# Leaky ReLU of a feed-forward with one operand taken from PSUM, in two halves

## The reference

```python
# layer 0, after a deformable convolution with 4 groups x 9 points, a batch norm and a gate s
x3 = x2 * s[:, None, None, :]
hmid = jax.nn.leaky_relu(jnp.einsum('nhwc,oc->nhwo', x3, fc1_w) + fc1_b, SLOPE)   # 256 -> 1024, SLOPE = 0.01
m = jnp.einsum('nhwc,oc->nhwo', hmid, fc2_w) + fc2_b                              # 1024 -> 256
return (inp + m).transpose(0, 3, 1, 2)
```

## Time and profile before

| | |
|---|---|
| median of 3 runs | 7485.81 us (7482.09 to 7492.41) |
| the profiled execution | 7487.15 us |
| its span, from the first to the last instruction | 7485.3 us |
| mean granted TensorE clock (1 is 2.4 GHz) | 0.745 |
| VectorE busy | 5173.2 us, 69% |
| GpSimd busy | 4751.4 us, 63% |
| TensorE busy | 3828.6 us, 51% |
| ACT busy | 1072.8 us, 14% |

### The profile page before, as it was taken

One profiled execution on the slowest core, in us unless ns is written; L12 is line 12 of the kernel. 1 busy time (PEld: TensorE's weight loads), 2 busy tenths in 40 slices (PEclk: granted clock), 3 DMA queues, 4 the chain that ended last, 5 costly groups with the idle time before them and its releaser, 6 DMA issues.

```text
span 7485.3 us, 45646 instructions
## 1 busy us (share of the span) xinstructions
PE 3828.6 (51%) x10560; PEld 2011.8 (27%) x10560; DVE 5173.2 (69%) x5212; ACT 1072.8 (14%) x1619; POOL 4751.4 (63%) x4676
## 2 busy tenths in 40 slices
PE   5243142351475526632764346426656652589957
PEld 3121021220232214411322124213223431234523
DVE  3778778786777768866777679767777975432545
ACT  1110100000111002211110022101001210121333
POOL 0577777777777777777777777777777777200000
PEclk9666576675687767866887678768878876799978
DMA  6373563754433333355333333553333355201067
GB/s 167 109 206 98 178 183 99 220 149 138 148 122 124 101 103 116 123 203 173 122 123 113 103 111 123 191 181 128 122 113 105 122 175 178 79 34 36 34 177 166
DMA packets 681090, 991.26 MB, mean 132 GB/s; under 512 B 413984, under 2 KB 483616, under 8 KB 665248
## 3 DMA queue, kind: packets, MB, share of 16 engines
q0 software_dynamic: 221184, 604.27, 25.2%
q1 hardware_dynamic: 459808, 385.87, 17.2%
HBM read 792.21 MB, written 197.59 MB: 132 GB/s over the span
## 4 chain that ended last, share of the span: by engine, by line
POOL 49%; issue 22%; PE 13%; DVE 9%; DMA 4%; SPq 2%; ACT 1%; DVEq 0%; POOLq 0%; ACTq 0%
POOL ring L369 48%; PE PS L690 12%; DVE ring L1337 3%; DVE dbuf L1343 2%; DMA img<-d_dram 2%; DMA ring<-table,idx_stage 1%; SPq L483 1%; ACT img L1059 1%; DMA cb<-o_dram 1%; DVE sm L1749 0%; DMA o_dram<-img 0%; POOL idx_stage L385 0%; DMA d_dram<-dbuf 0%; SPq L618 0%; SPq L639 0%
## 5 line engine op out<-in xcount | busy, mean ns | idle before, releaser
L369 POOL DMA_INDIRECT ring<-table,idx_stage x4608 | 4720.1, 1024 | 1435.2 <-issue 1370.1
L1343 DVE TENSOR_REDUCE dbuf<-ring 128x64 f32<-128x2304 f32 x512 | 2070.1, 4043 | 45.9 <-DMA d_dram<-dbuf 18.4
L1337 DVE TENSOR_TENSOR ring<-ring,wt 128x576 f32<-128x576 f32 x2048 | 1414.0, 752 | 973.7 <-DMA ring<-table,idx_stage 855.1
L690 PE MATMUL PS<-img,wb_sb 128*128 128x512 f32 (+1 forms) x3328 | 1646.8, 656 | 468.9 <-DVE img L1402 296.4
L690 PE MATMUL PS<-img,wa_sb 128*128 (+1 forms) x1984 | 931.4, 631 | 666.5 <-DVE img L1723 248.3
L690 PEld LDWEIGHTS PS<-img,wb_sb 128*128 128x128 f32 x3328 | 694.9, 213 | 1387.0 <-issue 1098.4
L690 PEld LDWEIGHTS PS<-img,wa_sb 128*128 128x128 f32 x1984 | 398.4, 203 | 1170.1 <-issue 1079.3
L690 PE MATMUL PS<-sm,params 128*128 128x4 f32 (+1 forms) x32 | 9.1, 355 | 863.1 <-DVE sm L1381 762.0
L690 PE MATMUL PS<-wa_sb,cb 128*128 128x108 f32 (+1 forms) x1024 | 238.8, 399 | 371.8 <-DVE cb L1402 371.8
L787 PE MATMUL PS<-params,img 128*128 128x128 f32 x256 | 62.9, 427 | 689.1 <-DMA img<-d_dram 689.1
L1059 ACT ACTIVATE img<-PS,sm 128x512 f32<-128x512 f32 x384 | 247.5, 680 | 1092.9 <-PE PS L690 1092.9
(11 more groups left out here) (191 smaller groups left out, 2977.5 us busy)
## 6 DMA issues: line engine op xcount, KB each, us to landing
ring<-table,idx_stage POOLq DMA_INDIRECT x4608, 2.9
table<-cb SPq DMA_DIRECT2D x128, 512.0 KB, 7.3
img<-y_dram SPq DMA_DIRECT2D x64, 512.0 KB, 6.6
q_dram<-img SPq DMA_DIRECT2D x32, 1024.0 KB, 4.3
img<-q_dram SPq DMA_DIRECT2D x32, 1024.0 KB, 6.9
img<-in_x SPq DMA_DIRECT2D x8, 2048.0 KB, 12.2
y_dram<-cb SPq DMA_DIRECT2D x64, 256.0 KB, 3.0
d_dram<-dbuf SPq DMA_DIRECT2D x128, 128.0 KB
```

What stands on the lines that cost most here:

```text
L369: nc.gpsimd.indirect_dma_start(out=ring[:, g, p * CORNERS * GC:(p + 1) * CORNERS * GC], out_offset=None, in_=tab[b], in_offset=bass.Indire ...
L690: return nc.tensor.matmul(o, l, r, start=start, stop=stop, **kw)
L1337: last = vec.tensor_tensor(rg, rg, weights.unsqueeze(2).to_broadcast([P, n, GC]), ALU.mult)
L1343: vec.tensor_reduce(dbuf[:, j, g * GC:(g + 1) * GC], ring[:, g, :].rearrange("p (k c) -> p c k", c=GC), AX_X, ALU.add).then_inc(sem("ring_ ...
```

## The change

ACT writes 0.01 (z + b) in place of z + b: it takes `fb_low` = 0.01 `fb` as its bias and 0.01 as its scale. VectorE then takes z itself from PSUM, adds `fb` and writes the larger of that and ACT's value, bank by bank, so in two instructions of 128 x 512 in place of one of 128 x 1024. Since VectorE is now the last reader of these banks, `up(q)` waits for VectorE's step q-2 (gB), not for ACT's. `fb_low` is made beside `fb`, once for each image, with one wait more, and the tile of small values grows by its 8 columns.

```diff
--- before.py
+++ after.py
@@ -169,7 +169,7 @@
         cb = sb("cb", [P, 4 * 1024])
         stats = sb("stats", [P, KC * CHUNKS * 6])
         ostats = sb("ostats", [P, KC * B * CHUNKS * 6])
-        sm = sb("sm", [P, 496])
+        sm = sb("sm", [P, 504])
         PS = ctx.enter_context(nc.psum_tensor("PS", [P, 8, 512], F32))
 
         def v(name, k=None, rows=P):
@@ -190,7 +190,7 @@
         cb1 = small(2)
         rsum, xmean, s_hid, s_z, s_e, s_g, s_ga, s_gc = (small(2) for _ in range(8))
         rsums = small(KC * CHUNKS)
-        fb = small(8)
+        fb, fb_low = small(8), small(8)
         a_hid, m_hid, ang, sin_c, cos_c, mod = small(1), small(1), small(2), small(2), small(2), small(2)
         mz = small(2)
         U, V_ = small(18), small(18)
@@ -203,7 +203,7 @@
         e_sq, e_var, e_sd, e_s, e_t, e_s1 = (small(SETS) for _ in range(6))
         o_bn = small(2 * KC)
         obn4 = small(2 * SETS)
-        assert used[0] <= 496, used[0]
+        assert used[0] <= 504, used[0]
 
         coef = cb[:, 0:KC * K2 * K2]
 
@@ -821,7 +821,7 @@
                         n, c = i * 2 + (b * CHUNKS + h), i * 2 + h
 
                         def up(q):
-                            room(pe, "gZ", n * 4 + q)
+                            room(pe, "gB", n * 4 + q)
                             for j in range(2):
                                 for k in range(KC):
                                     at = k * 4 * C + (2 * q + j) * P
@@ -1159,7 +1159,7 @@
                             room(act, "gB", n * 4 + q)
                             for j in range(2):
                                 last = A_(i2[4 + q % 2][:, j * CHUNK:(j + 1) * CHUNK], PS[:, 2 * (q % 2) + j, :], ACT.Identity,
-                                          bias=fb[:, 2 * q + j:2 * q + j + 1])
+                                          bias=fb_low[:, 2 * q + j:2 * q + j + 1], scale=SLOPE)
                             last.then_inc(sem("gZ"), 1)
                 loop(ACT.Identity, f2)
                 barrier()
@@ -1614,7 +1614,8 @@
                 vec.tensor_tensor(s_ga, s_g, bninv[:, 4:6], ALU.mult)
                 vec.tensor_tensor(s_gc, s_g, bnsh[:, 4:6], ALU.mult).then_inc(sem("se_gate"), 1)
                 dve.wait_ge(sem("fc1_shift"), b + 1)
-                vec.tensor_tensor(fb, PS[:, 5, 0:FC], v("fc1_b"), ALU.add)
+                link(vec.tensor_tensor(fb, PS[:, 5, 0:FC], v("fc1_b"), ALU.add))
+                vec.tensor_scalar(fb_low, fb, SLOPE, None, ALU.mult)
                 for k in range(KC):
                     w_ = wb_sb[:, F_FC1 + k * 4 * C:F_FC1 + (k + 1) * 4 * C]
                     last = vec.tensor_scalar(w_, w_, s_ga[:, k:k + 1], None, ALU.mult)
@@ -1627,7 +1628,12 @@
                         for q in range(4):
                             done(dve, "gZ", n * 4 + q)
                             room(dve, "gD", n * 4 + q)
-                            leaky(i2[6 + q % 2], i2[4 + q % 2]).then_inc(sem("gB"), 1)
+                            for j in range(2):
+                                half = slice(j * CHUNK, (j + 1) * CHUNK)
+                                last = vec.scalar_tensor_tensor(out=i2[6 + q % 2][:, half], in0=PS[:, 2 * (q % 2) + j, :],
+                                                                scalar=fb[:, 2 * q + j:2 * q + j + 1],
+                                                                in1=i2[4 + q % 2][:, half], op0=ALU.add, op1=ALU.max)
+                            last.then_inc(sem("gB"), 1)
                             stream.give(1, 8)
                         done(dve, "gD", n * 4 + 3)
                         dve.wait_ge(sem(f"gYl{h}"), m * 16 + 16)
```

## The result

The changed kernel takes 7451.07 us (median of six runs, 7444.49 to 7458.92) where the kernel before takes 7482.69 us in the same comparison (six runs, 7476.07 to 7492.41): a ratio of 0.9957, 95% interval 0.9944 to 0.997. That is 31.6 us less, with 22 to 42 in the interval. The forecast was 18 us less, and the range ended at 7454. The kernel before was itself 3.1 us quicker in this comparison than the 7485.81 on which the range was built.

What follows compares the result with a forecast made beforehand. The prediction took GpSimd's gathers to bound three of four stretches, TensorE's matmuls the fourth. From 7487.15 us it took 19 for gathers, added 0.4 for bias and 0.5 for the fourth: 7469, or 7468 against the median; range 7454 to 7487.

Steps and rivals of the forecast that it cites:

- What bounds it: GpSimd's gathers bound the first three of four image stretches, 32 activation steps each; matmuls bound the fourth; VectorE has room.
- the term of 19 us: Gathers no longer held by L1402 in the first three stretches: 0.7 to 0.9 us per chunk, 17 to 21 for 24.
- The ceiling of 33 us: Upper bound on the gathers' saving: four gathers held by L1402 in one chunk, 1.38 us, over 24 chunks.
- The part given back: Gathers freed of L1402 reach the multiplies in another phase and are held there, so less than 33 us is saved.
- The coarse comparison: Mean gather 1032 ns against 1003 in a next-layer stretch without L1402: 25 us, of which something belongs to L1641.
- VectorE's step: 1.40 in place of 1.21 us per step, 6 us per stretch, free in the first three under waits for gathers.
- PSUM room: TensorE's up(q) now waits for VectorE's step q-2; down(q-2), queued ahead, waits for the same increment: nought.
- The fourth stretch: Bound by TensorE, without gathers; down(0) and down(3) may wait for VectorE's later step: 0 to 3 us, 0.5 taken.
- A: Freed gathers run into multiplies or L1641 at worse points, eating 14 of the 19 us: 7482; chance 0.20.
- B: No relief: bias pointer counts as second SBUF input, or holds have another cause: 7487 to 7490; chance 0.13.
- C: TensorE's clock in the fourth stretch falls from 0.99 to 0.84 through new waits: 40 us more, 7508; chance 0.05.
- D: The whole upper bound of 33 us is gained, freed gathers meeting no new hold: 7454; chance 0.05.

Runs made afterwards that it cites:

- the square of four: VectorE's step whole or in halves, in0 from SBUF or PSUM: whole/SBUF 7481 to 7490, halves/SBUF 7504, halves/PSUM 7451 and 7458, whole/PSUM 7453 us.
- the kernel with six parts: The changed kernel with the multiplies of a gathered unit (L1337) cut into six instructions of 128x384, not four of 128x576: 7428.47 us, 0.9921 of the kernel before.

## Why the prediction was right in kind and wrong in size

**What bounds it: right.** GpSimd's time in the three stretches fell and so did the kernel's; VectorE's rose in the first by 6 us, and by 45 with the step twice, for nothing.

**The gathers: the mechanism right, the size wrong.** This is the step that failed: the term of 19 us. It measured 30.8 us by the length of the three stretches, or 28.0 by holds; the 2.8 us between the two weren't traced. It was made from one chunk, times 24. That chunk was one of the quicker ones. It takes 47.96 us; over three profiles chunks three to eight take 48.43 with L1402 in the step and 47.06 with the operand from PSUM. So they save 1.37 us each, not 0.8, and 24.7 in the 18 of them. (The forecast of 47.96 - 0.8 = 47.16 us for a chunk after lies close to that mean, partly by luck: in its own trace the chunk that was read went from 47.96 to 47.38.) The first two chunks of a stretch are not such chunks at all, with some 41 and 43 us before; in the three stretches they save 6.2 us together. By holds, the 9 us that are missing lie in two places:

- The ceiling of 33 us was the same chunk's 1.38 us times 24. Over the whole run L1402's holds in the step are 37.2, 41.2 and 38.1 us in the three profiles, 38.8 on average.
- The part given back was taken as 14 us (33 - 19). It is 11: the holds of all lines in the three stretches fall from 76.0 to 48.0 us, by 28.0 and not by 38.8, since those of the multiplies rise from 36 to 47.

By units, the steps of the working did come true. Second unit: 0.59 and 0.09 in the changed kernel against 0.51 in all before, so nothing saved, as said. Third and fourth: 0.47 and 0.09. First: 0.45 and 0.08, where 0.36 or 0.54 was forecast. The coarse comparison that the prediction set aside as too high, 25 us from the mean gather of two stretches, was the better one, and still too low; it came from 279 gathers, not from four.

The Trainium skill ("SBUF — State Buffer", section "Who interferes with whom") says that an instruction with at most one SBUF input, outside the modes that use both ports, does not contend with GpSimd; the square of four agrees, 7451 to 7458 against 7481 to 7504 us. The same section reports that a `tensor_tensor` did not stall a DMA which GpSimd issues. That does not carry over to these gathers: the multiplies, of just that kind, hold them for 217 to 232 us of the run. That it is the gather's reading of its row numbers in SBUF which is held is likely, but no run here tests it.

**VectorE's step: right.** 739 ns and a pair of 1.40 us, hidden under the waits for gathers. Making it cheaper (7453.03) or leaving it out (7457.58) gives nothing.

**PSUM room, ACT: nought, right.** The wait alone gives 1.0001.

**The fourth stretch: right.** 224.5 us in place of 224.9. TensorE's weight loads now wait for VectorE's step 16 times and not 8, for 3.8 us in all and not 1.9, as the waits of the two kernels show (before, then after), and the idle time of a load ahead of its turn hides it.

```profile
PEld PS L690 <- DVE img L1402: 1.9, 8, 0.2
```

```profile
PEld PS L690 <- DVE img L1633: 3.8, 16, 0.2
```

**The rivals.** A (phases eat the gain) falls for this change: they took 11 of 39 us. It isn't empty, though: in the kernel with six parts two other lines took 27 of the 61 us by which the multiplies' holds fell. B (no relief) falls by the 0.95 us gathers across the step. C (the clock) falls: 0.99 here, and 0.99 with 24 waits of up to 1.6 us when the step is made twice. D (the whole of the upper bound, 33 us, 7454) is the nearest in number, but not in its reason: not all holds went, the bound was too small.

**The range** was built on the same chunk at both ends, so its low end shared the forecast's error. The 37 us of all 96 steps, which the same trace held, would have put the low end at some 7450 and the result inside; the 25 of the group's mean would only have moved the forecast, to 7462. The chances have a slip: four fifths of 0.57 and all of D are 0.51, not 0.52.

## What to carry to other kernels

Where GpSimd issues indirect DMAs and is the engine that ends last, look for VectorE instructions that read two tensors from SBUF: take one operand from PSUM where it lies there anyway, and cut the long ones into parts, since a hold mostly lasts to the end of the instruction. Parts that follow each other at once can still hold a gather across several of them (3.03 us for one), so look for that in the trace afterwards. Sum such holds over all instructions of a line before you put a price on them; one chunk can be the lucky one. And count what the freed work runs into next: cutting one line moved 27 us of holds to two others, and cutting the larger of those as well gave 40 us. First see that GpSimd is what ends last: on the other chip it wasn't.

## What the hardware showed that was not expected

- Halves from SBUF hold as much as the whole: 32.6 us in 91 gathers against 37.2 in 92, 0.36 us each against 0.40, though each half is only 0.74 us long. No pair holds two gathers; the first half has 34 of the 91 and the second 57, most of them begun within 0.3 us of its start. So the gain of a shorter instruction was lost because the gathers came early in it. Why they do wasn't tested.
- A hold of one gather can be 1.5 us, behind an instruction of 2.29, and 2.1 us across four multiplies that follow each other at once; the longest gather of the run with in0 from SBUF takes 4.15 us.
- More work on VectorE made the three stretches 15 us shorter (the step twice). That is half of what the change itself gained, and it was not foreseen.
- One instruction of 128x1024 with an operand from PSUM takes 1273 ns against 1215 from SBUF, and two halves 1.40 us.
